# A four-layer stack on one core: the last beat of a norm split into two beats, and the rope of batch 1 placed in front of the norm of batch 2

## The chip, the cores and the metric

One core of one Trainium2 chip runs the whole program. The metric is the device time of one execution in microseconds; lower is better. The kernel before takes 2440.07 us (median of 3 runs, 2438.58 to 2442.01).

## The reference, cut to what matters

`x` is 4 batches of 512 tokens and 512 channels, fp32. Four layers follow one another, each conditioned on a vector per batch:

```
L0: h = layernorm(x)*(1+scale)+shift ; q = h Wq ; kv = h Wkd ; k = kv Wku ; v = kv Wvu   (16 heads of 32, 4 k/v heads)
    rope(q), rope(k) ; softmax(q k' + block mask) v ; x += out Wo
L1: h = rms(x)*w*(1+t tw) ; q, k, v (8 heads of 64, 1 k/v head) ; rope ; softmax ; x += ctx Wo
    h = rms(x)*w2*(1+t tw2) ; x += (silu(h Wg) * (h Wu)) Wd
L2: h = ln(x)*(scale1+1)+shift1 ; qkv ; q, k to unit norm ; softmax ; x += (out Wproj)*gamma1
    h = ln(x)*(scale2+1)+shift2 ; x += (gelu(h Wfc1) Wfc2)*gamma2
L3: y = 8 experts (64 -> 256 -> 64, gelu) ; silu(ln(y)*(1+scale)+shift) out_W ; x += that
```

## The kernel before, in words

Everything is held with channels on the partitions: 512 channels are C = 4 channel tiles of 128, the 512 tokens of a batch are the free axis. A norm over channels is therefore a sum over partitions: GpSimd adds the four tiles (`xsum`, then `vsum` of the squares, three additions each, lines 278 to 287), TensorE sums over the partitions with a matrix of ones (`mean`, `var`, line 265), ScalarE takes squares (line 303) and the inverse root as log and exp (lines 311 and 316), VectorE centres (line 344) and multiplies (`scale`, line 364), and ScalarE adds the shift (`shift`, line 328; for the norm of L2 also the bias of the residual, `extra`, line 334). For L2 the normed values go out as a high and a low part (`rest`, line 348, on VectorE). An RMS norm has no mean and no shift.

Work is cut into small operations of one engine each. `Heads` is the main stream of an attention: for each batch 64 blocks of rows of one head, each with scores (TensorE, line 705), a masked row maximum (`max`, VectorE, line 785), exp (ScalarE, line 815), a transpose of the probabilities (`turn`, TensorE, line 713), a copy of it out of PSUM (`copy`, even blocks half on ScalarE, line 820, and half on VectorE, line 792), the product with V (`values`, line 729), a spread of the row sums (`spread`, line 739) and a division (`divide`, line 803). Everything else that an attention's neighbours need (the norm, the projections and the rope of the batches to come, the output projection of the batch before) is a side stream: `beats(b)` of a stage gives a list of beats, each a list of operations that are issued together. `weave` (line 880) lays the beats of a batch's side list evenly over the 64 points of its main stream, so the number of beats in the list sets where each of them lands. Each engine then runs its operations strictly in this order, and waits at an operation whose input is not there.

`SideNorm.beats` (lines 241 to 256) has for its last beat all four tiles: 4 `scale` (and 4 `shift`, and for L2 4 `rest` and 4 `extra`). The side list for the first attention, `sides01` (line 1492), has an entry for each m, the batches of L0 and then of L1 in turn. Its entry holds the norm of batch 1 (for m = 0 alone), the projections of batch m+1 (`pre(m + 1, 1)`), and then, mixed evenly by `among`, the output projection of the batch before, the rope of batch m+1 (`pre(m + 1, 2)`, 5 beats) and the norm of batch m+2 (`pre(m + 2, 0)`, 7 beats for a layer norm).

A rope turns 5 tiles: number 0 is K, numbers 1 to 4 are Q. For batch 0 TensorE swaps neighbouring channels with a permutation (line 453). For batch 1 and later ones the sync engine's DMA queue does it, two DMAs a tile (`swap`, line 1741); then VectorE multiplies by the sine (`sin`, line 468), GpSimd by the cosine and adds (`cos` line 480, `add` line 486). The swapped tiles stand in two buffers in turn, so swap 2 waits for add 0 and swap 4 for add 2. In L0 the turned K is then copied to 15 more places by 15 DMAs (line 1753). The queue's program is written out by hand:

```
swap 0, swap 1, wait for add 0, 15 copies of K, swap 2, swap 3, swap 4        (batch 1)
```

The lead, before the first attention, computes norm, projections and rope of batch 0 beside 12 blocks of a matrix-vector product for the conditioning (`ada`, lines 132 and 138); `fold` lays these over the beats of the lead. The MLPs and the last layer are ordered by lists of their own, in which `SideNorm.beats` is used in the same manner (norm1b, norm2b, norm3).

Of the kernel before, what the change touches and what calls it, by code (L numbers as in the profile page):

```python
# [16 lines left out]
C = D // P  # L17
# [212 lines left out]
class SideNorm:  # L230
# [10 lines left out]
    def beats(s, b):  # L241
        squares = [("act", "square", c) for c in range(C)]
        scales = [("dve", "scale", c) for c in range(C)]
        adds = [("pool", "vsum", i) for i in range(3)]
        tail = [adds, [], [("pe", "var", 0), ("act", "log", 0), ("act", "inverse", 0)]]
        if s.rms:
            return [squares] + tail + [scales]
        ends = [op for c in range(C) for op in (("dve", "scale", c), ("act", "shift", c))]
        if s.high:
            ends = [op for c in range(C + 1) for op in ([("dve", "scale", c), ("act", "shift", c)] if c < C else []) +  # L250
                    ([("dve", "rest", c - 1)] if c else [])]
        if s.extra:
            ends += [("act", "extra", c) for c in range(C)]
        return [[("pool", "xsum", i) for i in range(3)], [],
                [("pe", "mean", 0)] + [op for c in range(C) for op in (("dve", "centre", c), ("act", "square", c))]] \
            + tail + [ends]

    def reader(s, kind, index):
        return ("centre", C - 1) if kind == "mean" else ("log", 0)
# [610 lines left out]
def fold(parts, *streams):  # L870


    behind = {}
    for first, last, beats in streams:
        for i, ops in enumerate(beats):
            behind.setdefault(first + (2 * i + 1) * (last - first) // (2 * len(beats)), []).extend(ops)
    return [op for i, ops in enumerate(parts) for op in ops + behind.get(i, [])]
# [303 lines left out]
def conditioned_stack(nc, a, out):  # L1181
    ctx = ExitStack()
    with ctx:
# [284 lines left out]
        def beats(*parts):  # L1468
            return [ops for stage, b in parts for ops in
                    ([(stage, b, *op) for op in beat] for beat in stage.beats(b))]  # L1470
# [4 lines left out]
        def among(*parts):  # L1475

            placed = [((2 * i + 1) / (2 * len(part)), n, ops) for n, part in enumerate(parts)
                      for i, ops in enumerate(part)]
            return [ops for _, _, ops in sorted(placed, key=lambda entry: entry[:2])]

        def pre(m, *which):
            stages, b = pres[m] if m < 2 * B else ((), 0)
            return beats(*[(stages[i], b) for i in which if stages])
# [8 lines left out]
        sides01 = []  # L1492
        for m in range(2 * B - 1):
            late = beats(posts[m - 1]) if m else []
            sides01.append(([] if m else pre(1, 0)) + pre(m + 1, 1) + among(late, pre(m + 1, 2), pre(m + 2, 0)) + [[]])

        def mlp_norm(n, A, Bias, before_h, before_t, spare=(), **more):

# [18 lines left out]
                         extra=combc(5), high=lambda b, c: hNhigh[c // 2][:, c % 2, :],  # L1517
# [59 lines left out]
        for m in range(B - 1):  # L1577
            side = [] if m else [[]] * 4
            side += beats((norm2, m + 1)) + qk2.among(proj2, m + 1)
            if m:  # L1580
                late = beats((post2, m - 1))
# [371 lines left out]
```

How the kernel before makes its waits and increments, by code:

```python
def start_wait(k, e, at, *names, but={}):  # L38
    for name in names:
        n = at[name] - but.get(name, 0)
        if n > 0:
            e.wait_ge(k.done[name], n)
# [19 lines left out]
    def dve(s, k, e, b, kind, index, after):  # L64
        if kind == "negate":
            for due in after(s.name, b, "sin", 0):
                e.wait_ge(*due)
            e.tensor_scalar(k.table[:, 2, :], k.table[:, 1, :], -1.0, None, ALU.mult).then_inc(k.done["dve"], 1)
            return
        steps = [0]
        def inc(ins):
            steps[0] += 1
            ins.then_inc(k.s_angle, 1)
            e.wait_ge(k.s_angle, steps[0])
        e.wait_ge(k.l_pos, 16 * (B + 1))
        ang, kk, r = (k.work[:, i, :] for i in range(3))
        inc(e.tensor_copy(kk, k.pos))
        inc(e.tensor_scalar(ang, kk, k.freq[:, 0:1], None, ALU.mult))
# [12 lines left out]
    def act(s, k, e, b, kind, index, after):  # L93
        for due in after(s.name, b, "reduce", 0):
            e.wait_ge(*due)
        k.act_set = "sin"
        src, out = (k.work[:, 4, :], k.table[:, 1, :]) if kind == "sin" else (k.work[:, 5, :], k.table[:, 0, :])
        e.activation(out, src, ACT.Sin).then_inc(k.done["act"], 1)
# [22 lines left out]
    def pe(s, k, e, b, kind, j, after):  # L121
        bank = s.tab.claim(e, s, b, kind, j, after)
        if kind == "block":
            if j == 0:
                e.wait_ge(*s.first_loaded)
                e.wait_ge(*s.cond_loaded)
            if j == 4:
                for due in after(s.name, b, "silu", 0):
```

## Time and profile before

| | before |
|---|---|
| median of 3 runs | 2440.07 us |
| profiled execution, its own time | 2440.45 us |
| its span | 2438.7 us |
| TensorE busy | 2292.4 us (94%) |
| VectorE busy | 1210.7 us (50%) |
| ScalarE busy | 1071.2 us (44%) |
| GpSimd busy | 294.2 us (12%) |

The span is the time from the first to the last instruction in the trace; the time of the execution is 1.75 us longer. Shares are of the whole span. The stages lie one after the other: lead to 84 us, first attention (L0 and L1) 84 to 817, MLP of L1 to 1399, attention of L2 1399 to 1926, MLP of L2 to 2297, last layer to the end. A row of the timeline gives start, duration, engine, line, what is written and read, and in brackets the idle time before it with what ended it.

### The profile page before, as it was taken

What the parts mean: (1) busy time and instruction counts of PE and PEld (TensorE: products, weight loads), DVE (VectorE), ACT (ScalarE), POOL (GpSimd) and SP (SyncE); (2) the same over time, 40 slices, a digit from 0 to 9 for tenths busy, and PEclk for the clock granted to TensorE, in tenths of its full rate; (3) what the DMA queues carried; (4) which work ended last, traced back from release to release, by engine and by line L of the source; (5) the groups of instructions that cost most, each with busy time, mean ns of one, the idle gap of its engine ahead of it and who ended that gap; (6) DMA issues with size and microseconds to landing.
All of it is one profiled execution on the core that took longest, in us unless ns stands there. A gap on an engine that the chain in (4) does not pass through costs nothing.

```text
span 2438.7 us, 33137 instructions
## 1 busy us (share of the span) xinstructions
PE 2292.4 (94%) x13314; PEld 1510.6 (62%) x13314; DVE 1210.7 (50%) x2486; ACT 1071.2 (44%) x2417; POOL 294.2 (12%) x246
## 2 busy tenths in 40 slices
PE   6879999999999999999999989999998989999998
PEld 2445455455555687888877756565664568888633
DVE  2465564554457444433433355657477655444332
ACT  2465565544445221111113266656567652222473
POOL 3332121121021011000001010101010110000021
PEclk9899999999999999999999989999999999999999
DMA  9111011000010002110102211111110001000001
GB/s 334 58 39 34 6 48 35 23 20 20 22 40 26 31 26 74 56 65 26 35 7 78 78 51 54 42 47 44 61 36 19 27 26 35 21 15 1 1 18 52
DMA packets 59594, 105.60 MB, mean 43 GB/s; under 512 B 10576, under 2 KB 24160, under 8 KB 59440
## 3 DMA queue, kind: packets, MB, share of 16 engines
q1 hardware_dynamic: 58480, 101.02, 12.5%
q0 software_dynamic: 960, 2.45, 0.3%
q8 instruction: 106, 1.74, 0.3%
q14 instruction: 48, 0.39, 0.1%
HBM read 77.76 MB, written 10.49 MB: 36 GB/s over the span
## 4 chain that ended last, share of the span: by engine, by line
PE 83%; DVE 7%; ACT 6%; POOL 1%; issue 1%; SPq 1%; DMA 1%; POOLq 0%; DVEq 0%; ACTq 0%
PE banks L1100 35%; PE banks L403 21%; PE banks L713 8%; PE banks L705 6%; PE banks L729 5%; DVE sb_Pr L785 2%; ACT sb_Pr L815 2%; PE banks L265 1%; PE banks L739 1%; PE banks L529 1%; PE banks L611 1%; ACT sb_PT L820 1%; DVE sb_hN L364 1%; PE banks L619 1%; SPq L1753 1%
## 5 line engine op out<-in xcount | busy, mean ns | idle before, releaser
L1100 PE MATMUL banks<-sb_HH,sb_Ws 128*128 128x512 f32 x1536 | 492.1, 394 | 12.7 <-DVE sb_HL L990 7.3
L713 PEld LDWEIGHTS banks<-sb_ident,sb_Pr 128*128 128x128 f32 x2176 | 240.7, 142 | 208.3 <-issue 69.7
L713 PE MATMUL banks<-sb_ident,sb_Pr 128*128 128x128 f32 x2176 | 317.5, 283 | 40.5 <-DVE sb_PT L792 13.1
L1100 PEld LDWEIGHTS banks<-sb_HH,sb_Ws 128*128 128x128 f32 x1536 | 291.0, 189 | 77.8 <-issue 17.2
L815 ACT ACTIVATE sb_Pr<-sb_Pr,sb_nmax 128x512 f32<-128x512 f32 (+3 forms) x512 | 321.7, 635 | 28.2 <-DVE sb_nmax L785 28.2
L1100 PE MATMUL banks<-sb_hidH,sb_Ws 128*128 128x512 f32 x1024 | 331.0, 392 | 0.0
L785 DVE CUSTOM_DVE_ANT_0 sb_Pr<-banks,sb_bias 128x512 f32<-128x512 f32 (+3 forms) x512 | 273.2, 586 | 87.0 <-PE banks L705 83.4
L1100 PE MATMUL banks<-sb_HL,sb_Ws 128*128 128x512 f32 x768 | 301.0, 392 | 0.0
L820 ACT ACTIVATE sb_PT<-banks 128x512 f32<-128x512 f32 (+3 forms) x320 | 154.4, 528 | 303.0 <-PE banks L713 302.5
L792 DVE COPY sb_PT<-banks 128x512 f32<-128x512 f32 (+3 forms) x320 | 181.1, 603 | 179.4 <-PE banks L713 178.4
L705 PE MATMUL banks<-sb_R 32*128 32x512 f32 (+4 forms) x1280 | 212.0, 584 | 13.7 <-DMA sb_R<-sb_R 6.7
L1100 PEld LDWEIGHTS banks<-sb_hidH,sb_Ws 128*128 128x128 f32 x1024 | 192.3, 188 | 45.2 <-issue 3.8
L1100 PE MATMUL banks<-sb_hidL,sb_Ws 128*128 128x512 f32 x512 | 199.3, 389 | 0.0
L403 PE MATMUL banks<-sb_A,sb_W 128*128 128x512 f32 x384 | 176.1, 602 | 3.4 <-DVE sb_x L1369 2.3
L1152 DVE TENSOR_TENSOR sb_tiles<-sb_tiles,banks 128x512 f32<-128x512 f32 x64 | 44.0, 687 | 271.6 <-PE banks L1100 271.6
L729 PE MATMUL banks<-sb_PT,sb_V 128*32 128x256 f32 (+2 forms) x2304 | 168.6, 379 | 0.0
L1127 ACT ACTIVATE sb_hidH<-sb_tiles 128x512 fp32r<-128x512 f32 x128 | 81.0, 632 | 197.7 <-DVE sb_tiles L1152 195.7
L1100 PEld LDWEIGHTS banks<-sb_HL,sb_Ws 128*128 128x128 f32 x768 | 145.7, 190 | 30.9 <-issue 1.0
L403 PE MATMUL banks<-sb_hN,sb_W 128*128 128x512 f32 x320 | 146.1, 600 | 2.8 <-ACT sb_hN L328 1.4
L1122 ACT ACTIVATE sb_tiles<-banks,sb_cols 128x512 f32<-128x512 f32 x64 | 44.1, 689 | 237.5 <-PE banks L1100 237.5
L1171 DVE SCALAR_TENSOR_TENSOR sb_x<-banks,sb_mod,sb_x 128x512 f32<-128x512 f32 x128 | 95.8, 750 | 90.2 <-PE banks L1100 89.9
L1119 ACT ACTIVATE sb_tiles<-banks 128x512 f32<-128x512 f32 x64 | 38.2, 597 | 223.0 <-PE banks L1100 222.9
(141 smaller groups left out, 2795.6 us busy)
## 6 DMA issues: line engine op xcount, KB each, us to landing
sb_ring<-split_units SPq DMA_DIRECT2D x48, 512.0 KB, 3.3
sb_ropet<-sb_R SPq DMA_DIRECT2D x70, 128.0 KB, 2.0
sb_staged<-in_L_cond_Wfc SPq DMA_DIRECT2D x16, 512.0 KB, 4.4
sb_wada<-in_L_cond_Wada SPq DMA_DIRECT2D x6, 1024.0 KB, 6.2
split_units<-sb_unitpair SPq DMA_DIRECT2D x12, 512.0 KB, 2.9
sb_x<-in_x SPq DMA_DIRECT2D x4, 1024.0 KB, 9.8
sb_staged<-in_L_cond_Wg SPq DMA_DIRECT2D x8, 512.0 KB, 3.5
sb_staged<-in_L_cond_Wu SPq DMA_DIRECT2D x8, 512.0 KB, 4.5
```

Of the source, the lines that this page charges most:

```text
L403: mm = e.matmul(bank[:, columns], lhsT, rhs, start=start, stop=stop)
L705: mm = e.matmul(bank[:, 0:s.width(u)], s.q(b, c)[rows, i * P:(i + 1) * P], s.k(b, c)[rows, 0:s.width(u)], start=True, stop=True)
L713: mm = e.transpose(bank[:, j * P:(j + 1) * P], k.Pr[:, n % 6, j * P:(j + 1) * P], k.ident[:])
L729: mm = e.matmul(bank[rows, 2 * P * ip + skip:2 * P * (ip + 1)], s.v(b, j, s.vhead(c, hl)), s.PT[:, n % 2, hl, j, skip:2 * P], start=j == 0 ...
L785: ins = e.tensor_tensor_reduce(k.Pr[:, n % 6, 0:s.width(u)], S, k.bias[:, s.units[u][2], 0:s.width(u)], -1.0, 3.0e38, ALU.add, ALU.min, s. ...
L792: ins = e.tensor_copy(*s.turned(k, b, u))
L815: ins = e.activation(prob, prob if s.biased else k.bank(n % 4)[:, 0:s.width(u)], ACT.Exp, bias=s.stat(k, k.nmax, b, u), scale=-1.0 if s.bi ...
L820: ins = e.activation(*s.turned(k, b, u), ACT.Copy)
L1100: mm = e.matmul(bank, lhsT, rhs, start=i == 0, stop=i == len(mats) - 1)
L1122: ins = e.activation(k.tile(t), bank, ACT.Gelu_apprx_tanh, bias=s.hbias[:, f:f + 1], scale=1.0)
L1127: ins = e.activation(k.hidH[:, st % 2, t, :], k.tile(t), ACT.Copy)
L1171: ins = e.scalar_tensor_tensor(out=k.xs(q, m), in0=s.tab.at[(s.name, b, "down", index)], scalar=1.0 if s.gamma is None else s.gamma(q, m), ...
```

## The change

The last beat of every norm becomes two beats of two channel tiles each. Only the L2 norm of batch 0 keeps one beat. Where there are `extra` operations, two of them now stand in the first half and two in the second. In `sides01[0]` the five beats of the rope of batch 1 now stand as a block in front of the eight of the norm of batch 2, which were mixed with them before. No operation is added or taken away; the list of each attention batch has one or two beats more, so all side beats land at slightly other points.

```diff
         if s.rms:
-            return [squares] + tail + [scales]
+            return [squares] + tail + [scales[:2], scales[2:]]
         ends = [op for c in range(C) for op in (("dve", "scale", c), ("act", "shift", c))]
         if s.high:
             ends = [op for c in range(C + 1) for op in ([("dve", "scale", c), ("act", "shift", c)] if c < C else []) +
                     ([("dve", "rest", c - 1)] if c else [])]
+        half = 5 if s.high else 4
         if s.extra:
-            ends += [("act", "extra", c) for c in range(C)]
+            extras = [("act", "extra", c) for c in range(C)]
+            ends = ends[:half] + extras[:2] + ends[half:] + extras[2:]
+            half += 2
         return [[("pool", "xsum", i) for i in range(3)], [],
                 [("pe", "mean", 0)] + [op for c in range(C) for op in (("dve", "centre", c), ("act", "square", c))]] \
-            + tail + [ends]
+            + tail + ([ends[:half], ends[half:]] if b or not s.high else [ends])
...
-            sides01.append(([] if m else pre(1, 0)) + pre(m + 1, 1) + among(late, pre(m + 1, 2), pre(m + 2, 0)) + [[]])
+            sides01.append(([] if m else pre(1, 0)) + pre(m + 1, 1) +
+                       (among(late, pre(m + 1, 2), pre(m + 2, 0)) if m else pre(1, 2) + pre(2, 0)) + [[]])
```

Lines after the edit are 3 or 4 higher in the changed kernel. What the change does to the order of the engines is shown at three places. The first is VectorE in the first attention, batch 0, around the multiplications by the sine of batch 1 (`sb_ropet<-sb_ropet,sb_sin`). Before, number 0 stands behind four row maxima, number 1 behind four more (numbers 128 to 135) and a division, and number 2 behind four copies of transposes, the centring of the next norm and four more maxima:

```order
125 L468 TENSOR_TENSOR sb_ropet<-sb_ropet,sb_sin 128x512
126 L797 RECIPROCAL sb_rsum<-sb_sums 128x16
127 L792 COPY sb_PT<-banks 128x128 x2
128 L785 ISA sb_Pr,sb_nmax<-banks,sb_bias 128x384
...
136 L803 TENSOR_TENSOR sb_A<-sb_A,banks 128x512
137 L468 TENSOR_TENSOR sb_ropet<-sb_ropet,sb_sin 128x512
138 L792 COPY sb_PT<-banks 128x2x128 x2
139 L344 TENSOR_TENSOR sb_hN<-sb_x,banks 128x512 x4
140 L785 ISA sb_Pr,sb_nmax<-banks,sb_bias 128x512
...
148 L792 COPY sb_PT<-banks 128x3x128 x2
149 L468 TENSOR_TENSOR sb_ropet<-sb_ropet,sb_sin 128x512
150 L785 ISA sb_Pr,sb_nmax<-banks,sb_bias 128x128
```

The same place in the changed kernel (here `max` is line 788, the sine line 471):

```order
118 L471 TENSOR_TENSOR sb_ropet<-sb_ropet,sb_sin 128x512
119 L788 ISA sb_Pr,sb_nmax<-banks,sb_bias 128x256
...
127 L471 TENSOR_TENSOR sb_ropet<-sb_ropet,sb_sin 128x512
128 L800 RECIPROCAL sb_rsum<-sb_sums 128x16
129 L795 COPY sb_PT<-banks 128x128 x2
130 L471 TENSOR_TENSOR sb_ropet<-sb_ropet,sb_sin 128x512
131 L788 ISA sb_Pr,sb_nmax<-banks,sb_bias 128x384
...
139 L471 TENSOR_TENSOR sb_ropet<-sb_ropet,sb_sin 128x512
140 L806 TENSOR_TENSOR sb_A<-sb_A,banks 128x512
141 L795 COPY sb_PT<-banks 128x2x128 x2
142 L471 TENSOR_TENSOR sb_ropet<-sb_ropet,sb_sin 128x512
143 L788 ISA sb_Pr,sb_nmax<-banks,sb_bias 128x512
```

Number 2 now stands in front of the maxima of width 384, 8 maxima and 4 centrings earlier than before; numbers 3 and 4 follow four and no maxima later.

The second place is ScalarE in the attention of L2, at the end of the norm of batch 2 (`sb_hNhigh` is its high part, `sb_x<-sb_x,sb_comb` the extra). Before:

```order
623 L311 ACTIVATE sb_Pb<-banks,sb_eps 128x512
624 L316 ACTIVATE sb_Pb<-sb_Pb 128x512
625 L820 ACTIVATE sb_PT<-banks 128x4x128 x2
626 L815 ACTIVATE sb_Pr,sb_sums<-sb_Pr,sb_nmax 128x512 x2
627 L328 ACTIVATE sb_hNhigh<-sb_hN,sb_mod 128x512 x4
628 L334 ACTIVATE sb_x<-sb_x,sb_comb 128x512 x4
629 L815 ACTIVATE sb_Pr,sb_sums<-sb_Pr,sb_nmax 128x512 x2
```

And changed:

```order
630 L314 ACTIVATE sb_Pb<-banks,sb_eps 128x512
631 L319 ACTIVATE sb_Pb<-sb_Pb 128x512
632 L331 ACTIVATE sb_hNhigh<-sb_hN,sb_mod 128x512 x2
633 L337 ACTIVATE sb_x<-sb_x,sb_comb 128x512 x2
634 L823 ACTIVATE sb_PT<-banks 128x4x128 x2
635 L818 ACTIVATE sb_Pr,sb_sums<-sb_Pr,sb_nmax 128x512 x2
636 L331 ACTIVATE sb_hNhigh<-sb_hN,sb_mod 128x512 x2
637 L337 ACTIVATE sb_x<-sb_x,sb_comb 128x512 x2
638 L818 ACTIVATE sb_Pr,sb_sums<-sb_Pr,sb_nmax 128x512 x2
```

Two shifts and two extras now stand in front of a copy of transposes (line 823) that stood ahead of all eight before.

The third place is the end of VectorE's program, in the last layer (`sb_Y` with `sb_comb,sb_Pb` is the scale of norm 3 of batch 3, `sb_x<-banks` the residual of the output projection). Before:

```order
1930 L344 TENSOR_TENSOR sb_Y<-sb_Y,banks 128x512 x4
1931 L1599 SCALAR_TENSOR_TENSOR sb_x<-banks,sb_cols,sb_x 128x512 x3
1932 L364 SCALAR_TENSOR_TENSOR sb_Y<-sb_Y,sb_comb,sb_Pb 128x512 x4
1933 L1599 SCALAR_TENSOR_TENSOR sb_x<-banks,sb_cols,sb_x 128x512 x4
1934 L1183 UNCONDITIONAL_BRANCH
```

And changed:

```order
1949 L347 TENSOR_TENSOR sb_Y<-sb_Y,banks 128x512 x4
1950 L1603 SCALAR_TENSOR_TENSOR sb_x<-banks,sb_cols,sb_x 128x512 x2
1951 L367 SCALAR_TENSOR_TENSOR sb_Y<-sb_Y,sb_comb,sb_Pb 128x512 x2
1952 L1603 SCALAR_TENSOR_TENSOR sb_x<-banks,sb_cols,sb_x 128x512
1953 L367 SCALAR_TENSOR_TENSOR sb_Y<-sb_Y,sb_comb,sb_Pb 128x512 x2
1954 L1603 SCALAR_TENSOR_TENSOR sb_x<-banks,sb_cols,sb_x 128x512 x4
```

The scales of two tiles moved in front of the third residual of batch 2, those of the other two stayed behind it.

## Rows read from the trace of the kernel before

**Rows 1.** The page, busy time (share of the span), and the chain that ended last.

```profile
PE 2292.4 (94%) x13314; PEld 1510.6 (62%) x13314; DVE 1210.7 (50%) x2486; ACT 1071.2 (44%) x2417; POOL 294.2 (12%) x246
...
PE 83%; DVE 7%; ACT 6%; POOL 1%; issue 1%; SPq 1%; DMA 1%; POOLq 0%; DVEq 0%; ACTq 0%
```

**Rows 2.** Timeline of PE, lead: last projection and first turn of batch 0, first scores.

```profile
66.77 1.02 PE L403 MATMUL banks<-sb_t,sb_W 128*128 128x512 f32 x2
67.73 1.06 PE L132 MATMUL banks<-sb_wada,sb_cond 128*32 128x512 f32 x8
...
85.83 0.81 PE L705 MATMUL banks<-sb_R 32*128 32x128 f32 x8 [6.70 <-DMA sb_R<-sb_R]
```

**Rows 3.** Timeline of PE, 104 to 162 us.

```profile
105.94 3.67 PE L403 MATMUL banks<-sb_hN,sb_W 128*128 128x512 f32 x8 [1.40 <-ACT sb_hN L328]
...
160.96 1.85 PE L705 MATMUL banks<-sb_R 32*128 32x256 f32 x8 [4.65 <-DVE sb_nmax L785]
```

**Rows 4.** Timeline of SP's queue, 136 to 165 us.

```profile
145.57 11.02 SPq L1753 DMA_DIRECT2D sb_R<-sb_R  x15
156.69 7.74 SPq L1741 DMA_DIRECT2D sb_ropet<-sb_R  x6
```

**Rows 5.** Timeline of DVE, 138 to 164 us: sines 0 and 2.

```profile
142.12 0.86 DVE L468 TENSOR_TENSOR sb_ropet<-sb_ropet,sb_sin 128x512 f32<-128x512 f32 x1 [0.57 <-DMA sb_ropet<-sb_R]
...
160.00 0.69 DVE L468 TENSOR_TENSOR sb_ropet<-sb_ropet,sb_sin 128x512 f32<-128x512 f32 x1 [6.24 <-DMA sb_ropet<-sb_R]
```

**Rows 6.** Timeline of POOL, 138 to 176 us: cosine 2, addition 2.

```profile
160.05 1.77 POOL L480 TENSOR_TENSOR sb_R<-sb_R,sb_cos 128x512 f32<-128x512 f32 x1 [11.37 <-DMA sb_ropet<-sb_R]
161.96 1.27 POOL L486 TENSOR_TENSOR sb_R<-sb_R,sb_ropet 128x512 f32<-128x512 f32 x1
```

**Rows 7.** Windows: length, busy PE, PEld, DVE, ACT, POOL; granted clock, DMA share.

```profile
147.50:161.00 13.50, 6.71 (x62) 4.33 (x61) 7.26 (x20) 6.96 (x17) 2.13 (x2) 0.92 0.39 109
161.00:179.60 18.60, 14.23 (x138) 7.71 (x138) 14.28 (x46) 13.66 (x41) 11.28 (x9) 0.87 0.04 14
```

**Rows 8.** Timeline of PE, 178 to 410 us.

```profile
179.65 1.94 PE L713 MATMUL banks<-sb_ident,sb_Pr 128*128 128x128 f32 x8 [2.73 <-DVE sb_PT L792]
...
234.31 0.30 PE L713 MATMUL banks<-sb_ident,sb_Pr 128*128 128x128 f32 x1 [1.75 <-ACT sb_t L303]
...
407.76 1.63 PE L739 MATMUL banks<-sb_ident,sb_rsum 128*32 128x128 f32 x32 [2.23 <-ACT sb_PT L820]
```

**Rows 9.** Timeline of ACT, 396 to 409 us: its idle time and the four squares.

```profile
401.67 0.28 ACT L820 ACTIVATE sb_PT<-banks 128x128 f32<-128x128 f32 x1 [2.96 <-PE banks L713]
...
405.26 2.18 ACT L303 ACTIVATE sb_t<-sb_x 128x512 f32<-128x512 f32 x4
```

**Rows 10.** Timeline of PE, attention of L2 and MLP of L2.

```profile
1431.96 1.12 PE L265 MATMUL banks<-sb_t,sb_ones 128*128 128x512 f32 x2 [1.47 <-POOL sb_t L287]
...
1556.70 0.47 PE L403 MATMUL banks<-sb_hNhigh,sb_ring 128*128 128x512 f32 x1 [0.99 <-DVE sb_hNlow L348]
...
1995.30 0.77 PE L1100 MATMUL banks<-sb_HH,sb_Ws 128*128 128x512 f32 x1 [6.81 <-DVE sb_HL L990]
```

**Rows 11.** Timeline of ACT, 1554 to 1842 us: extras, and shifts of batch 3.

```profile
1559.20 2.55 ACT L334 ACTIVATE sb_x<-sb_x,sb_comb 128x512 f32<-128x512 f32 x4
...
1835.56 2.71 ACT L328 ACTIVATE sb_hN<-sb_hN,sb_mod 128x512 f32<-128x512 f32 x4
```

**Rows 12.** Timeline of PE, 2400 to 2434 us.

```profile
2402.70 1.12 PE L265 MATMUL banks<-sb_t,sb_ones 128*128 128x512 f32 x2 [1.61 <-POOL sb_t L287]
...
2417.34 15.67 PE L403 MATMUL banks<-sb_Y,sb_Wout 128*128 128x512 f32 x32 [2.35 <-ACT sb_Y L328]
```

**Rows 13.** Timeline of DVE, 2400 to 2434 us: the residual that waits, then the scales.

```profile
2415.03 0.75 DVE L1599 SCALAR_TENSOR_TENSOR sb_x<-banks,sb_cols,sb_x 128x512 f32<-128x512 f32 x1 [3.54 <-PE banks L403]
2415.70 2.73 DVE L364 SCALAR_TENSOR_TENSOR sb_Y<-sb_Y,sb_comb,sb_Pb 128x512 f32<-128x512 f32 x4
2422.74 0.75 DVE L1599 SCALAR_TENSOR_TENSOR sb_x<-banks,sb_cols,sb_x 128x512 f32<-128x512 f32 x1 [4.32 <-PE banks L403]
```

## The prediction

> **What bounds the kernel now.** I read the page first: TensorE is busy 94% of the span and makes 83% of the chain that ended last [rows 1]. So the span is TensorE's work plus its idle time, and since the change adds and removes no operation, it can only move idle time, and the half-clock stretches that follow it. Idle time of the other engines counts only where TensorE waits for it. I therefore went through the timelines: each stop of TensorE in the lead, the first attention, the attention of L2 and the last layer [rows 2, 3, 8, 10, 12], and for each the engine it waited for [rows 4 to 6, 9, 11, 13], with the new order laid beside them. All sums are made against the profiled execution, 2440.45 us; the median of the runs is 2440.07, 0.38 less, which I don't correct for. A measurement of this kernel tells some 0.2% (4.9 us) from no change.
>
> **1. The rope of batch 1 (the place that decides).** The DMA queue issues 15 copies of K from 145.57 on, for 11.02 us, and only behind them swap 2, at 156.69 [rows 4]. Sine 2 is ready to run at 160.00, after VectorE stood idle 6.24 us at it, and GpSimd 11.37 us at cosine 2 [rows 5, 6]. Nothing in this chain is moved by the change: it starts at addition 0, which needs sine 0, and that waits for its own DMA until 142.12 in either order [rows 5]. What changes is what stands behind sine 2 on VectorE. Before, VectorE had done the maxima of 8 more score blocks, and TensorE had work until 156.3; it stood 4.65 us, and scores began again at 160.96 [rows 3]. Now sine 2 comes before the maxima of blocks 40 to 43, so the PSUM banks for scores 44 stay full until it is done: TensorE stops where scores 44 stood, at 147.5, and goes on at about 161. It thus does after 161 what it did in these 13.5 us before: 6.71 us of busy time [rows 7]. On top, sine 4 now stands ahead of the maxima of blocks 44 to 47 with swap 4 behind addition 2 at 163.2 [rows 6] (about 2.8 us to landing, so 166.0), and the mean of the next norm needs three additions of GpSimd that now stand behind all of the rope: from addition 2, four more operations of 1.27 and three for the norm give about 172. I lay the new order over these times and get scores 52 at 174.5 against 160.96, +13.5. Some of it comes back: until 179.6 TensorE was busy only 14.23 of 18.6 us [rows 7], since it stood at turns and at the variance for VectorE and GpSimd, whose sines, centring and additions are now done earlier or later. The stop of 2.73 at 179.65 [rows 8] shrinks, and I get that turn at about 191.2. Term: **+11.6**. Bounds: +7.5, if only the busy time of 6.71 and small change is pushed out and everything else is caught up; +14, if nothing comes back.
>
> The clock here: the window 147.5 to 161.0 had a granted clock of 0.92 and the next 0.87 [rows 7], so a stretch at 1.2 GHz follows the stop of 4.65 us already, and the term counts it once, as before. The Trainium skill ("TensorE: Matmul & The Clock Gate", the section on HAM oscillation) says that a wait for a DMA between bursts of matmuls lets the clock fall, so that each next burst starts at half rate; this speaks against the change, which makes two bursts with a wait before each out of one. The row shows one stretch for one wait; by the page's rule there would be a second.
>
> **2. The lead.** One more block of `ada` with its turn (eight matmuls 1.06, eight 1.05, about 2.0 together [rows 2]) now stands before the last projection at 66.77 that K's rope starts from. The chain from there to scores 0 at 85.83 (idle 6.70 for the copies of K [rows 2]) is all latency, but the block filled time elsewhere in it, and ScalarE's and the permutation's places take up part. Term: +0.9 (0 to 2.0).
>
> **3. Projections of batch 1.** TensorE waited 1.40 for a shift [rows 3]. Two shifts now come sooner, but the turn in front waits for a copy behind them: +1.0, less 0.5 at a later turn. Term: +0.5 (-1 to +1.5).
>
> **4. Rest of the first attention.** The stop at turn 60 of batch 1 is like that of 179.65: a copy of VectorE behind four scales. With two it halves, about -1.3. The stop of 1.75 at 234.31 [rows 8] is filled by a matmul group that moved in front, -1.9, and sine 0 of batch 2 waits before the copies now, +1.2: -2.0. In batch 2 the four squares of a norm (2.18 together [rows 9]) go in front of ScalarE's `out` and copies: spread 0 then waits 1.5, and a lower clock may follow: +2.3. In batch 3 the reverse: the four squares at 405.26 hold up the copies, and TensorE stands 2.23 at 407.76 [rows 8, 9]; now they go into ScalarE's idle 2.96 before 401.67 [rows 9]. The wait goes, and with it the slow matmuls behind it: -3.6 (-2.2 without the clock). Norm 1 in the attention of L1, with copies behind two scales in place of four: -0.6. Term: **-3.9** (-6 to 0).
>
> **5. Attention of L2.** Batch 0: the mean comes earlier and the wait of 1.47 for the variance [rows 10] goes, with part of the waits behind it; against it two shifts and extras ahead of a copy: -1.5. Batches 1 and 2: at 1556.70 the projection waited for low parts [rows 10]. It waited 0.99 there and in the same way for the tiles behind it, some 3 us in all in each batch. These go, but ScalarE's copy of transposes now stands behind two shifts and two extras (half of 2.55 and of 2.71 [rows 11], 2.6 together), of which some 1.7 shows at a turn: -1.5 each. Batch 3: ScalarE has the same sum of shifts (2.71 [rows 11]), extras and exps before the copy that TensorE waits for; the wait moves by two turns: +0.5. Term: **-4.0** (-7 to +1).
>
> **6. MLP of L2.** TensorE's stop of 6.81 at 1995.30 [rows 10] ends when the last low part of batch 3 is there, behind the shifts and extras on ScalarE. An activation, with a load of its function table, now stands between them and before shift 0, so high and low parts come about 1.5 to 2.5 later. Term: +2.3 (0.5 to 5).
>
> **7. Last layer.** TensorE stood 2.35 at 2417.34 for shift 0 of batch 3 [rows 12]. Its scale ran at 2415.70, behind a residual that waited 3.54 for TensorE [rows 13], though its input was there more than 2 us before. Now two scales go ahead of that residual, so the first two tiles are ready when TensorE comes, and the others follow by about 2417 and 2418: no idle time, 2.35, and no slow matmuls: the first eight of the 32 ended at 2422.74 [rows 13], 5.4 after 2417.34, the other 24 took the remaining 10.3 of 15.67 [rows 12], 3.4 each eight. The tiles' own latency takes back about 0.5 of the sum 2.35 + 2.0. Term so far -3.8. The wait of 1.61 for the squares' sum of batch 2 [rows 12] shrinks: -0.9. Term: **-4.7** (-6 to -2).
>
> The MLP of L1 and the rest: 0; TensorE is fed there by matmuls of its own with no side beat in front of them that is waited for.
>
> Sum: 11.6 + 0.9 + 0.5 - 3.9 - 4.0 + 2.3 - 4.7 = **+2.7**, so 2440.45 + 2.7 = 2443.1, rounded 2443.
>
> **The rivals.** (a) *Slower: attention of L2 is bound by ScalarE, so nothing comes back there.* Batch 3 shows it already: 2.71 of shifts and 2.55 of extras [rows 11] stand before a copy in any order, and a split changes only which turn waits. If batches 0 to 2 behave so, term 5 is +0.5 and the sum 7.2: 2447.7; with the rope's term at 14 as well, 2450. It decides once the new stop behind two shifts and two extras is over 3 us a batch. Against it: TensorE's waits in batches 1 and 2 were for low parts made by VectorE, not for a copy. Chance 0.30.
> (b) *Slower by the clock.* Two stops in the rope, at scores 44 and at the mean, give two stretches at 1.2 GHz where there was one. The eight matmuls behind 2417.34 took 5.4 after their stop against 3.4 for the others [rows 12, 13], half as much again; over the 6.71 us of work [rows 7] between the two stops that is +3.3: 2446.4. It decides if the second stop is as long as the one before 160.96 that lowered the clock. I expect half of that. Chance 0.10. This is how it would come out by the page's rule named under 1.
> (c) *Faster: the rope's wait costs no more than before.* If in the end the time until 179.65 is bound by VectorE (14.28 of 18.6 us [rows 7]) and GpSimd (11.28), work taken over early leaves less after 161, and the term falls to 6: 2437.5, and with full gains in terms 5 and 7, 2433. For it: sine 3, sine 4 and divisions are done sooner. Against it: VectorE stands idle from about 146 to 160 now, 7.26 us of its work [rows 7] pushed behind 160. Chance 0.15.
> (d) *It does nothing*: a beat of two is followed at once by the other two on an in-order engine, so the waits only change name, and the rope's block costs as much as the norms give back. Within 1 us of before. Chance 0.10.
>
> **How the numbers follow.** The main case (0.35) is the sum, 2443, by itself 2438 to 2448. With (a) to (d) around it the 8 in 10 reach from 2434 to 2451: below lies the extreme of (c), above that of (a) with the rope at its upper bound. Slower by over 4.9 us (from 2445) takes most of (a), half of (b) and a quarter of the main case: 0.39. Faster (below 2435.2) is the lower half of (c) and the main case's tail: 0.15. Within: 0.46.
>
> **What would show it.** Right: in the changed profile a stop of TensorE of 12 to 14 us that begins near 148 and ends near 161, with VectorE idle for the same time before its third sine; a second one at the mean; turn 60 at 189 to 194; no stop over 1 us at the squares of batch 3; no idle time before the final 32 matmuls. The loss to 192 us should be 10 to 15 us, and all that follows should give back 7 to 12. Wrong: if the queue's swap 2 is issued before 156; if TensorE's time to 192 us grows by under 7 us; or if waits of 2 us and more appear in each batch of the attention of L2 at a turn, which makes it (a).

## The result, and the profile after

The changed kernel takes 2447.26 us (median of 7 executions, 2439.35 to 2450.6); the kernel before, on the same chips, 2438.58 (7 executions, 2437.14 to 2442.91). The ratio is 1.0024, 95% interval 1.0013 to 1.0036: slower by some 6 us. The profiled execution of the changed kernel took 2446.37 us against 2440.45 before, +5.9.

The page of the changed kernel, busy time and the chain that ended last, against [rows 1]:

```profile
PE 2293.0 (94%) x13314; PEld 1516.1 (62%) x13314; DVE 1219.4 (50%) x2486; ACT 1070.2 (44%) x2417; POOL 297.5 (12%) x246
...
PE 83%; ACT 6%; DVE 6%; POOL 2%; DMA 1%; SPq 1%; issue 1%; DVEq 0%; POOLq 0%; ACTq 0%
```

Counts and TensorE's busy time are the same; idle time and clock moved. To see where, I took the start of the same operation of TensorE in both traces at each stage's border. Each line is what that stretch added to the changed kernel:

| stretch (step of the prediction) | predicted | by the two profiles |
|---|---|---|
| lead, to scores 0 (2) | +0.9 | +6.7 |
| to scores 40 of batch 0 (3) | +0.5 | +1.6 |
| to turn 60 of batch 0, the rope (1) | +11.6 | +10.3 |
| rest of the first attention and the start of the MLP of L1 (4) | -3.9 | -1.2 |
| MLP of L1 | 0 | -2.0 |
| attention of L2, to turn 60 of its batch 3 (5) | -4.0 | -7.3 |
| MLP of L2, to the first matmul of the last layer (6) | +2.3 | +5.5 |
| last layer (7) | -4.7 | -7.7 |
| sum | +2.7 | +5.9 |

The row for the MLP of L1 says nothing of the change: in fourteen profiles of kernels whose order there is nearly the same, that stretch took 551.3 to 555.3 us, with a mean granted clock of 1.000 to 0.994.

**The rope.** Four views of the changed kernel around it; lines are 3 or 4 higher than before. The DMA queue, 140 to 182 us (15 copies of K, then swaps 2 to 4), against [rows 4]:

```profile
153.06 10.72 SPq L1757 DMA_DIRECT2D sb_R<-sb_R  x15
163.88 7.07 SPq L1745 DMA_DIRECT2D sb_ropet<-sb_R  x6
```

VectorE's sines 1 to 3, against [rows 5]:

```profile
152.44 1.13 DVE L471 TENSOR_TENSOR sb_ropet<-sb_ropet,sb_sin 128x512 f32<-128x512 f32 x1 [0.57 <-DMA sb_ropet<-sb_R]
166.51 0.69 DVE L471 TENSOR_TENSOR sb_ropet<-sb_ropet,sb_sin 128x512 f32<-128x512 f32 x1 [12.43 <-DMA sb_ropet<-sb_R]
169.03 1.26 DVE L471 TENSOR_TENSOR sb_ropet<-sb_ropet,sb_sin 128x512 f32<-128x512 f32 x1
```

TensorE, against the 4.65 us in [rows 3]; the first row is turn 38, the second turn 39 with the stop before it, the third scores 44, the last the mean of the next norm:

```profile
157.03 0.69 PE L716 MATMUL banks<-sb_ident,sb_Pr 128*128 128x128 f32 x2
170.94 0.69 PE L716 MATMUL banks<-sb_ident,sb_Pr 128*128 128x128 f32 x2 [13.21 <-DVE sb_A L806]
171.56 2.09 PE L708 MATMUL banks<-sb_R 32*128 32x512 f32 x8
...
180.15 1.13 PE L268 MATMUL banks<-sb_t,sb_ones 128*128 128x512 f32 x2 [0.98 <-POOL sb_t L290]
```

And the windows of the changed kernel, with columns as in [rows 7]:

```profile
158.00:171.00 13.00, 0.06 (x1) 0.07 (x1) 4.49 (x12) 2.50 (x8) 4.30 (x3) 0.50 0.30 88
171.00:198.00 27.00, 21.93 (x202) 12.36 (x202) 21.08 (x62) 20.53 (x57) 12.16 (x10) 0.88 0.03 10
```

The queue does what it did, 7 to 8 us later with everything else. VectorE stands 12.43 us at sine 2 and did 4.49 us of work in 13, and TensorE 0.06 us. It stops one turn earlier than I said: turn 39 needs a division that stands behind sine 3.

**The lead.** Scores 0 starts at 92.58 against 85.83 [rows 2]. The idle time before it is nearly the same (6.84 and 6.70 us); what differs is the granted clock from 36 to 50 us: 0.50, which is 1.2 GHz throughout, against 0.88. Changed kernel, then before:

```profile
92.58 0.81 PE L708 MATMUL banks<-sb_R 32*128 32x128 f32 x8 [6.84 <-DMA sb_R<-sb_R]
...
36.00:50.00 14.00, 14.00 (x40) 6.54 (x41) 3.04 (x6) 5.11 (x8) 0.00 (x0) 0.50 0.95 287
```

```profile
36.00:50.00 14.00, 14.00 (x58) 5.44 (x57) 2.95 (x6) 6.18 (x10) 0.00 (x0) 0.88 1.04 320
```

**The attention and the MLP of L2.** TensorE in the changed kernel. In batch 1 the waits for low parts from 1556.70 on [rows 10] have become one wait for a copy (1566.92). In batch 3 there are two long waits, at turns 18 and 39 (1846.40 and 1888.79). In the MLP there is a wait at the variances of batch 2 and of batch 3 (1961.44 and 1989.12):

```profile
1566.92 1.06 PE L716 MATMUL banks<-sb_ident,sb_Pr 128*128 128x128 f32 x8 [1.49 <-ACT sb_PT L823]
...
1846.40 1.94 PE L716 MATMUL banks<-sb_ident,sb_Pr 128*128 128x128 f32 x8 [2.63 <-ACT sb_PT L823]
...
1888.79 1.11 PE L716 MATMUL banks<-sb_ident,sb_Pr 128*128 128x128 f32 x4 [3.73 <-DVE sb_A L806]
...
1961.44 1.17 PE L268 MATMUL banks<-sb_t,sb_ones 128*128 128x512 f32 x2 [2.40 <-POOL sb_t L290]
...
1989.12 1.60 PE L268 MATMUL banks<-sb_t,sb_ones 128*128 128x512 f32 x2 [2.31 <-POOL sb_t L290]
...
2007.93 0.77 PE L1103 MATMUL banks<-sb_HH,sb_Ws 128*128 128x512 f32 x1 [5.15 <-DVE sb_HL L993]
```

The same stretch before: turns 16 and 40 of batch 3, and the only wait at a variance.

```profile
1838.26 1.90 PE L713 MATMUL banks<-sb_ident,sb_Pr 128*128 128x128 f32 x8 [2.22 <-ACT sb_hN L328]
...
1884.26 1.23 PE L713 MATMUL banks<-sb_ident,sb_Pr 128*128 128x128 f32 x8 [2.43 <-DVE sb_PT L792]
...
1979.16 1.12 PE L265 MATMUL banks<-sb_t,sb_ones 128*128 128x512 f32 x2 [1.25 <-POOL sb_t L287]
```

**The last layer.** TensorE, against [rows 12], and VectorE, against [rows 13]:

```profile
2412.10 1.13 PE L268 MATMUL banks<-sb_t,sb_ones 128*128 128x512 f32 x2 [0.74 <-POOL sb_t L290]
...
2426.64 12.29 PE L406 MATMUL banks<-sb_Y,sb_Wout 128*128 128x512 f32 x28 [0.17 <-ACT sb_Y L331]
```

```profile
2422.38 1.42 DVE L367 SCALAR_TENSOR_TENSOR sb_Y<-sb_Y,sb_comb,sb_Pb 128x512 f32<-128x512 f32 x2 [1.49 <-ACT sb_Pb L319]
2424.43 0.75 DVE L1603 SCALAR_TENSOR_TENSOR sb_x<-banks,sb_cols,sb_x 128x512 f32<-128x512 f32 x1 [0.64 <-PE banks L406]
2425.09 1.41 DVE L367 SCALAR_TENSOR_TENSOR sb_Y<-sb_Y,sb_comb,sb_Pb 128x512 f32<-128x512 f32 x2
```

Two scales run in front of the residual as soon as the inverse is there, and of the 2.35 us of idle time 0.17 is left.

### The profile page after: what moved, and what is told of

Same layout as the page of the kernel before. It is cut to its first block, busy times and chain, and to the rows that moved or that the text cites. A ratio compares the mean times of both kernels' runs of the same rounds, so it can differ in the third digit from the quotient of the medians.

```text
span 2444.6 us, 33118 instructions
## 1 busy us (share of the span) xinstructions
PE 2293.0 (94%) x13314; PEld 1516.1 (62%) x13314; DVE 1219.4 (50%) x2486; ACT 1070.2 (44%) x2417; POOL 297.5 (12%) x246
## 4 chain that ended last, share of the span: by engine, by line
PE 83%; ACT 6%; DVE 6%; POOL 2%; DMA 1%; SPq 1%; issue 1%; DVEq 0%; POOLq 0%; ACTq 0%
PE banks L1103 35%; PE banks L406 21%; PE banks L716 8%; PE banks L708 6%; PE banks L732 5%; ACT sb_Pr L818 2%; DVE sb_Pr L788 2%; PE banks L268 1%; PE banks L742 1%; PE banks L532 1%; ACT sb_PT L823 1%; PE banks L614 1%; PE banks L622 1%; ACT sb_t L306 1%; SPq L1757 1%
## 5 line engine op out<-in xcount | busy, mean ns | idle before, releaser
L716 PE MATMUL banks<-sb_ident,sb_Pr 128*128 128x128 f32 x2176 | 322.6, 286 | 61.5 <-DVE sb_A L806 28.7
```

The lines of the kernel that those rows point to most:

```text
L716: mm = e.transpose(bank[:, j * P:(j + 1) * P], k.Pr[:, n % 6, j * P:(j + 1) * P], k.ident[:])
```

## The experiments

In all of them a method `split(s, b)` of `SideNorm` decides for which norm and batch the last beat is cut. Lines are up to 12 higher than before. "us" are medians; ratios are to the kernel before with 95% intervals, and a gain or loss in us is the ratio's. The rope block is in the kernel only where the text says so.

**All norms split, no rope block.**

```diff
-                       (among(late, pre(m + 1, 2), pre(m + 2, 0)) if m else pre(1, 2) + pre(2, 0)) + [[]])
+                       among(late, pre(m + 1, 2), pre(m + 2, 0)) + [[]])
```

> All norms split in two beats, but the rope of batch 1 mixed with the norm of batch 2 as before. Theory A (the terms of the prediction): the rope block costs about 10 us at batch 1's sines, everything else is the split. Then this kernel has TensorE's turn 60 of batch 0 of the first attention at most 3 us later than before once the lead is taken off, no stop over 5 us near scores 44, and a time of 2437 us (10 below the changed kernel's 2447). Rival B (the split, not the block, makes the long stop, since all side beats move to other points): the stop of 12 to 14 us stays and the time is 2445 or more.

Measured: 2430.67 us, ratio 0.9963 (0.9950 to 0.9976), 9 us faster than before. No stop over 2.7 us near there; from scores 40 to turn 60 of batch 0 it gains 2.4 us on before. Theory A holds, and rival B falls; the time is lower than it said.

**The rope block alone**, in the changed kernel with its block:

```diff
     def split(s, b):
-        return True
+        return False
```

> No norm split, only the rope of batch 1 placed as a block in front of the norm of batch 2. Theory A: +10 us against before, 2448 to 2449, with a stop of TensorE of 12 to 14 us before VectorE's third sine and one at the mean; lead as before (scores 0 at 85.8 us). Rival B: under +4 us, since without the split the block lands at other points and is hidden.

Measured: 2450.18 us, ratio 1.0040 (1.0028 to 1.0053), +9.8 us. TensorE in this kernel:

```profile
168.31 0.69 PE L722 MATMUL banks<-sb_ident,sb_Pr 128*128 128x128 f32 x2 [13.11 <-DVE sb_A L812]
...
178.71 1.12 PE L274 MATMUL banks<-sb_t,sb_ones 128*128 128x512 f32 x2 [0.67 <-POOL sb_t L296]
```

From scores 40 to turn 60 it loses 10.8 us. The stop is the block's alone. The lead was not as before: scores 0 came at 90.5, although its order in the lead is that of before.

The two parts don't quite add up: -9.0 for all norms split and +9.8 for the block make +0.8, and the changed kernel has +5.9. The intervals (3 us to each side for each) just allow it. Against the kernel with all norms split the block costs 12.7 us from scores 40 to turn 60 by the profiles, and about 15 us by the two ratios.

**Only the norm in the lead split**, `return s.name == "norm0" and b == 0`.

> Only the norm of batch 0 of the first layer, in the lead, is split. The changed kernel's profile reaches scores 0 at 92.6 us against 85.8, and TensorE's granted clock stays at 0.5 from 36 to 49 us against 36 to 39. Theory L (the order of the lead's blocks keeps the clock low): scores 0 at 91 to 93 us in this kernel too, and a time of +5 to +7 us, 2444 to 2446. Rival C (chance of that one execution): scores 0 within 1.5 us of 85.8, and a time within 2 us of before.

Measured: scores 0 at 92.12 as in the changed kernel, yet 2440.03 us, ratio 1.0003 (0.9991 to 1.0014). The profile agrees with theory L and the time refutes it.

**The order of before, profiled again.**

> The order of the kernel before, unchanged on every engine: a second profile of it. Theory C (the state of the clock in the lead and in batch 0 of the attention of L2 differs from one execution to the next): scores 0, at 85.8 us in the first profile, or the step from scores 0 of the attention of L2 to its batch 1, 139.7 us, differs by over 2 us. Rival L (both are set by the order of the program): both within 1 us.

One execution, 2442.77 us. TensorE's first scores and the window of the lead:

```profile
90.61 0.81 PE L714 MATMUL banks<-sb_R 32*128 32x128 f32 x8 [6.81 <-DMA sb_R<-sb_R]
...
36.00:50.00 14.00, 13.85 (x41) 6.48 (x42) 3.04 (x6) 5.11 (x8) 0.10 (x1) 0.55 0.95 284
```

The same program reached scores 0 4.8 us later, with a clock of 0.55 in place of 0.88, and went from scores 0 of batch 0 of the attention of L2 to scores 0 of batch 1 in 130.1 us in place of 135.0 (the 139.7 of the expectation reaches to a later turn). Theory C holds. The other profiles show the same two clocks. Where the lead is not split, scores 0 stands at 85.8 to 86.8 us with the high clock (three profiles) and at 90.2 to 90.8 with the low one (six); where it is split, at 87.2 (one, the run with three swaps ahead below) and at 91.1 to 93.2 (four). So the split lead costs 0.3 to 3.1 us at a like clock, and the larger part of the +6.7 in the table is the clock of these two executions.

**Only norms 2 and 3 split**, `return s.name in ("norm2", "norm3")`.

> Only norm 2 (batches 1 to 3) and norm 3 (last layer) split. Theory A, with the sizes that the changed profile shows: the attention of L2 gives back 7 us and the last layer up to 7: 2425 to 2431. As predicted before the result: 2430. Rival D (the waits only change their name): within 2 us of before.

Measured: 2423.34 us, ratio 0.9923 (0.9911 to 0.9936), 18.7 us faster. By its profile batches 1 and 2 of the attention of L2 give 3.6 us each, the last layer 7.7. These two norms alone bring twice what the change with all norms split brings.

**Only norm2b split**, `return s.name == "norm2b"`, and **only its batches 0 and 1**, `return s.name == "norm2b" and b < 2`.

> Only the norm of the MLP of L2 (norm2b) split. Theory A, from the profiles of the changed kernel, of the kernel with every norm split and of the one with norms 2 and 3 alone: this norm costs 4 us at the end of the attention of L2 (waits at turns 18 and 39 of its batch 3) and 6 us in the MLP of L2: 8 to 12 us more than before, 2449 to 2453. As predicted before the result: +2.8 (0.5 from its share in the attention, 2.3 in the MLP). Rival: the difference between those kernels is the clock's, under 3 us.

> Only batches 0 and 1 of norm2b split: they lie in batch 3 of the attention of L2; the order of the MLP of L2 is that of before. The kernel with all four split was 8 us slower than before, 3.3 of it in the attention by the profile. Theory A: +2 to +4 us, 2441 to 2443, with TensorE's waits at turns 18 (2.6 us) and 39 (3.7 us) as there and none of 2.4 us at the variances in the MLP. Rival: within 1 us of before, and the whole cost is the MLP's.

Measured: 2448.87 us, ratio 1.0033 (1.0019 to 1.0047), +8.0; and 2442.60 us, ratio 1.0016 (1.0001 to 1.0031), +3.9. TensorE in the second one, batch 3 of the attention; in its MLP the one wait at a variance is the 1.25 us of before:

```profile
1848.30 1.06 PE L722 MATMUL banks<-sb_ident,sb_Pr 128*128 128x128 f32 x8 [2.63 <-ACT sb_PT L829]
...
1889.07 1.12 PE L722 MATMUL banks<-sb_ident,sb_Pr 128*128 128x128 f32 x4 [3.73 <-DVE sb_A L812]
```

So the cost is in part in the attention and in part in the MLP: by the profile of the first one 3.4 and 5.6 us. The intervals allow 0.2 to 7.6 us for the part in the attention.

**Swap 2 ahead of the copies of K**, in the changed kernel and in the one before. The queue waits for the same addition 0 first:

```diff
                 done("rope0", b, "add", 0)
+                for g in range(2, 3) if b else ():
+                    swap(rope0, b, g)
                 heads = k.R[:, b % 2, 1, C - 1, :]
...
-                for g in range(2, 5) if b else ():
+                for g in range(3, 5) if b else ():
                     swap(rope0, b, g)
```

> The changed kernel with one thing else in the DMA queue: swap 2 of batch 1 is issued before the 15 copies of K (it waits for the same addition 0), swaps 3 and 4 behind them as before. Theory A (the long stop is VectorE standing at sine 2, for a DMA that the queue issues behind 11 us of copies): sine 2 runs near 149 us in the frame of before, the stop of 13.2 us at turn 39 goes or moves to sine 3, which stands behind four more maxima, and is then under 10 us; time 2 to 10 us less than the changed kernel. Rival (the stop is VectorE's and GpSimd's own work in this order): no more than 2 us less.

> The kernel before with swap 2 of batch 1 issued before the copies of K. Theory A: VectorE's idle 6.24 us at sine 2 and TensorE's 4.65 us before scores 52 go; sine 3, whose swap still comes behind the copies, is later in VectorE's order; time 3 to 6 us less than before. Rival: the copies end some 1.3 us later and nothing else changes, within 2 us.

Measured, changed kernel: 2445.59 us, ratio 1.0027 (1.0016 to 1.0037), no gain (the changed kernel's is 1.0024). Its sines 2 and 3 on VectorE, and TensorE's stop:

```profile
157.54 0.69 DVE L477 TENSOR_TENSOR sb_ropet<-sb_ropet,sb_sin 128x512 f32<-128x512 f32 x1 [3.60 <-DMA sb_ropet<-sb_R]
169.04 0.69 DVE L477 TENSOR_TENSOR sb_ropet<-sb_ropet,sb_sin 128x512 f32<-128x512 f32 x1 [8.90 <-DMA sb_ropet<-sb_R]
```

```profile
170.38 0.69 PE L722 MATMUL banks<-sb_ident,sb_Pr 128*128 128x128 f32 x2 [12.90 <-DVE sb_A L812]
```

Sine 2 runs 9 us earlier, but turn 39 waits for the division behind sine 3, and sine 3's swap is still behind the copies. My time for this run was wrong for that reason. In the kernel before: 2434.59 us, ratio 0.9978 (0.9966 to 0.9989), -5.4 us, as theory A said; there the sine that waits (2.84 us) has 8 maxima ahead of it that keep TensorE busy.

**Swaps 2, 3 and 4 ahead of the copies in the changed kernel** (`range(2, 5)` ahead, none behind).

> The changed kernel with swaps 2, 3 and 4 of batch 1 all issued before the 15 copies of K. With swap 2 alone moved, the stop stayed (12.9 us at turn 39), now behind sine 3, whose swap the queue still issued after the copies. Theory A: with all three ahead, no sine waits for more than 4 us, the stop of 13 us goes down to under 4, and the time is 8 to 13 us below the changed kernel: 2434 to 2439. Rival (in this order VectorE and GpSimd are themselves too slow, or the copies, now some 8 us later, hold up the scores of batch 1): less than 4 us below.

Measured: 2433.21 us, ratio 0.9983 (0.9970 to 0.9997), some 10 us below the changed kernel by the ratios. The DMA queue, sine 4 (no sine from number 2 on waited over 1.6 us), and the rest of the stop at turn 39:

```profile
142.46 13.21 SPq L1751 DMA_DIRECT2D sb_ropet<-sb_R  x10
155.72 10.80 SPq L1765 DMA_DIRECT2D sb_R<-sb_R  x15
```

```profile
157.12 1.34 DVE L477 TENSOR_TENSOR sb_ropet<-sb_ropet,sb_sin 128x512 f32<-128x512 f32 x1 [0.42 <-DMA sb_ropet<-sb_R]
```

```profile
155.69 0.54 PE L722 MATMUL banks<-sb_ident,sb_Pr 128*128 128x128 f32 x2 [2.88 <-DVE sb_A L812]
...
164.88 1.13 PE L274 MATMUL banks<-sb_t,sb_ones 128*128 128x512 f32 x2 [2.19 <-POOL sb_t L296]
```

13.21 us are 2.88. Most of the block's cost was the queue's order: swaps behind 15 copies that nobody needs before batch 1. Some 10 of its about 15 us come back. The rest is in part in the stops of 2.88 and 2.19 above: against the kernel with all norms split and no block this one is 3.6 us longer from scores 40 to turn 60 by the profiles, and some 5 us in all (the intervals of the two ratios just overlap).

**Norms 2 and 3 split with one swap, and with three swaps, ahead of the copies**: a version that beats both.

> Norms 2 and 3 split, no rope block, swap 2 ahead of the copies. If the two effects (-18.7 and -5.4 us) add up: 2415 to 2418, under both kernels. Rival: with the waits of one gone, the other brings less, 2420 or more.

> The same with swaps 2, 3 and 4 ahead of the copies. Theory A: sine 3, which waited 2.84 us with swap 2 alone ahead, doesn't wait, TensorE's 1.04 us before turn 52 goes: 1 to 3 us less than with one swap ahead, if the copies of K still land before the scores of batch 1 want them. Rival: swaps 3 and 4 wait for additions 1 and 2, the copies come 6 to 8 us later, and scores 0 of batch 1 wait for them: slower than with one swap ahead.

Measured: 2415.60 us, ratio 0.9906 (0.9885 to 0.9927), and 2411.09 us, ratio 0.9887 (0.9863 to 0.9911), 27 us under the kernel before. The gains add up within the intervals (-22.9 us for the first, -18.7 and -5.4 apart). The rival's wait exists too, TensorE at scores 0 of batch 1 in the second:

```profile
175.47 0.50 PE L714 MATMUL banks<-sb_R 32*128 32x128 f32 x8 [2.30 <-DMA sb_R<-sb_R]
```

but it takes the place of the 2.73 us at turn 60 that was there [rows 8]. The two intervals overlap, so that three swaps beat one is likely and not shown.

## Why the prediction came out right, step by step

The measured 2447.26 lies in the range of 2434 to 2451, and slower had a chance of 0.39; the point, 2443, was 4 low. The likeliest case was "within 0.2%", and the ratio, 1.0024, is just beyond it.

The rope, the largest term, was understood. That the sum came out 3.2 us from the profile's is luck for the rest: the lead missed by 5.8 us, step 4 by 2.7, and steps 5, 6 and 7 by -3.3, +3.2 and -3.0, which cancel. Of the signs that were named, the loss to turn 60 is 11.9 us with the lead taken off (10 to 15 foreseen; 18.6 with it), and what follows gives back 12.7 (7 to 12 foreseen).

**1, the rope: right in mechanism and size.** Predicted +11.6, measured +10.3 in the changed profile and +9.8 (6.8 to 12.9) as a kernel of its own; against the kernel with all norms split it is 12.7 by the profiles. The stop was foreseen as 12 to 14 us beginning near 148 in the time of before; it is 13.21 us, beginning at 157.7, which is near 149.5 with the 8 us by which all is later there. With three swaps ahead 2.88 us of it are left. Only the place was off by one turn: TensorE doesn't stop at scores 44 with full banks but at turn 39, for the division behind sine 3. That step, left out, is also why the run with one swap ahead went wrong.

**2, the lead: size right at a like clock** (0.3 to 3.1 for +0.9, by profiles alone). What I didn't see is that the profile of before was an execution with the clock high there. The run with the lead's norm alone split shows no difference beyond its interval of -2 to +3.

**4, the rest of the first attention: wrong, -3.9 for -1.2.** The step that failed is batch 1: the stop of 1.75 at 234.31 [rows 8] that I let a matmul group fill was not lost but moved. It is now 1.77 at turn 20, and the group that was to fill it, the output projection, itself waits 1.70. Changed kernel:

```profile
239.16 0.63 PE L716 MATMUL banks<-sb_ident,sb_Pr 128*128 128x128 f32 x4 [1.77 <-DVE sb_PT L795]
...
254.92 3.70 PE L406 MATMUL banks<-sb_A,sb_W 128*128 128x512 f32 x8 [1.70 <-DVE sb_hN L347]
```

From turn 60 of batch 0 to that of batch 1, -2.0 was predicted and +1.2 measured. With all norms split and no block, the whole stretch of step 4 has +0.5. Batch 3 did as I said: the stop of 2.23 [rows 8] is gone, worth 3.6 from batch 2's turn 60 to batch 3's. That gain is sure, 3.3 to 3.8 in all four profiles with all norms split and in no other; the rest of step 4 is no larger than what the two profiles of the kernel before differ by there (2.7 from turn 60 of batch 1 to that of batch 2, 2.8 in the attention of L1).

**5, the attention of L2: two sizes off.** In batches 1 and 2 the gain is 3.6 us each where I took 1.5, though the new wait at the copy is 1.49 (1.7 foreseen). TensorE's idle time fell by 1.7 us in each (6.82 to 5.12 in batch 1), near my 1.5; the other 1.9 us is in no stop that the profile shows, at a granted clock of 1.00 in both, and its cause stays open. In batch 3 the loss is 4.6 for +0.5 (3.0 in the kernel with all norms split, whose order there is the same). I had ScalarE's copy right (2.22 becomes 0.90 and 2.63); the step left out is VectorE at turn 39, 3.73 us, where 2.43 stood at turn 40. Batch 0 gives 4.7 in these two profiles, but the second profile of the kernel before does the same: without norm 2 split it takes 135.0 us in three profiles and 130.1 in four, with it 130.2 to 131.6 in all seven. So the split gives nothing against the better of the two; whether it keeps the worse one away is not shown. So rival (a) was right about batch 3 and wrong about 1 and 2.

**6, the MLP of L2: mis-sized, +2.3 for +5.5.** The activation ahead of shift 0 does what I said. What I left out is the variance: it now stands before groups of matmuls that had covered it, with 2.40 and 2.31 us of idle time in place of 1.25. With the last stop of 5.15 for 6.81 that is only +1.8 in stops. The rest is clock: behind each of the two waits the granted clock is 0.66 over five us, which is some 3.4 us at 1.2 GHz and costs half of that; behind the 1.25 before it is 1.00. It is the same in all five profiles with norm2b split in every batch (+5.5 to +5.6), and -0.3 where only its batches 0 and 1 are. Changed kernel, then before, columns as in [rows 7]:

```profile
1961.00:1966.00 5.00, 4.56 (x11) 3.35 (x12) 1.41 (x2) 2.60 (x3) 0.30 (x1) 0.66 0.83 237
1989.00:1994.00 5.00, 4.88 (x13) 3.36 (x13) 1.42 (x2) 2.60 (x3) 0.07 (x1) 0.66 0.02 3
```

```profile
1979.00:1984.00 5.00, 4.84 (x19) 3.68 (x20) 2.70 (x5) 4.88 (x7) 0.10 (x1) 1.00 0.00 2
```

**7, the last layer: mis-sized the other way, -4.7 for -7.7.** The end gives -3.5 (-3.8 foreseen), and the wait for the sum of squares fell from 1.61 to 0.74, the -0.9 foreseen. What I had left at nothing is the stop in expert 1, which fell from 2.70 to 1.89; with it a stretch of low clock goes, eight matmuls taking 3.37 before and 1.94 after. Up to the first output projection that is -2.1; another 1.2 lies in small pieces behind it. All seven profiles with norm 3 split show this stop at 1.9 with the high clock behind it and -7.7 for the layer. Of the seven without, six have the low clock behind the 2.70 and one (only norm2b split) the high one. Before, then changed:

```profile
2329.47 3.37 PE L619 MATMUL banks<-sb_experts,sb_W 128*64 128x512 f32 x8 [2.70 <-ACT sb_experts L632]
```

```profile
2342.64 1.94 PE L622 MATMUL banks<-sb_experts,sb_W 128*64 128x512 f32 x8 [1.89 <-ACT sb_experts L635]
```

**Rival (b)**, two stretches of low clock at the rope for two stops: the second stop, at the mean, was 0.98 us. The window 158 to 171 has 0.50 and the next 27 us 0.88, that is some 6.5 us at 1.2 GHz in the time when TensorE works; before it was 0.92 and 0.87 in 32 us [rows 7], about as much. The rule of the Trainium skill ("TensorE: Matmul & The Clock Gate", the section on HAM oscillation) that a wait between bursts lets the clock fall agrees with both traces. In the changed kernel no second stretch followed the 0.98 us at the mean: from 178 to 197 us the granted clock is 1.00. The run with three swaps ahead has two stops, 2.88 at turn 39 (to 155.69) and 2.19 at the mean (to 164.88), and its clock did fall behind each:

```profile
156.00:159.00 3.00, 3.00 (x14) 1.33 (x13) 2.30 (x5) 0.00 (x0) 2.52 (x3) 0.50 0.46 128
159.50:165.00 5.50, 3.31 (x40) 2.33 (x40) 3.43 (x16) 5.15 (x16) 5.10 (x5) 1.00 0.39 97
167.00:172.00 5.00, 4.20 (x33) 1.77 (x35) 4.26 (x14) 4.37 (x14) 3.77 (x3) 0.50 0.07 18
```

So the condition of (b), a second stop as long as the first of before, was not met in the changed kernel; that a second stop can bring a second stretch is shown by these rows. **(c)** fell with the block alone at +9.8. **(d)** fell with norms 2 and 3 alone at -18.7.

## What to carry to other kernels

Before you move a step to an earlier place in an in-order engine, follow each of its inputs back to the queue that sends it: a consumer that is moved ahead of a transfer's landing gains nothing and holds up everything behind it, and here moving swaps ahead in the DMA queue gained where the new order lost. Splitting a long beat helped in norms 2 and 3, whose next consumer takes it tile by tile. It cost in norm2b, where the split put two shifts and extras ahead of a copy that TensorE waits for and moved the variance away from the matmuls that had covered it. So test a general rule norm by norm. Price each stop with the clock behind it, in both directions.

## What the runs showed of the hardware that was not expected

The same program differs from one execution to the next by more than most steps of this change: the kernel before took 2430.28 to 2446.38 us in 28 executions. Two profiles of it differ by 4.8 us in the lead, where TensorE's clock rose at 40 us in one and near 48 in the other, and by 4.9 us the other way in batch 0 of the attention of L2. TensorE's idle time is nearly the same in both (29.3 and 29.0 us in the lead, 11.0 and 11.7 in that batch). What decides it is open; the profiles show only that the old and the new order of the lead have each been seen with the high and with the low clock. A difference between two single profiles is worth little here until it is found in a third.

In two places the clock behind a stop changed the time by more than the stop itself did: by some 3.4 us against 1.8 in the MLP of L2, and by 1.4 against 0.8 in expert 1. It fell to 1.2 GHz behind the 2.31 and 2.40 us at the variances and the 2.19 us at the mean above, and stayed at 2.4 GHz behind the 1.25 us at the variance of before and the 1.89 us in the last layer. The idle time alone doesn't decide it: behind the same stop of 2.70 us in expert 1 it fell in six profiles and stayed high in one.
